# A decoder layer with eight experts on one core: the experts' units numbered the other way, w2 loaded in rows of 8 KB, the first layer's weights standing with a step of eight, and some stores and row copies moved to ScalarE

## What is computed

```python
x = x + self_attention(layernorm(x))            # 16 heads of 16, 3-D rope, softmax over 256 keys, output matrix Wo
x = x + cross_attention(ctx, ctx, layernorm(x))  # keys and values straight from ctx, masked, output W_fc.T
x = x + ffn(layernorm(x))
# ffn, with 8 experts of 1024 units, and 4 "languages":
router_logits = x @ router_w.T + router_b + 0.1 * expert_weights(softmax(x @ lang_w.T + lang_b))
top_p, top_i  = top_k(softmax(router_logits), 2);  top_p = top_p / top_p.sum()
h             = gelu(einsum('bsd,edh->bseh', x, w1) + b1)      # 256 -> 1024, exact gelu
expert_out    = einsum('bseh,ehd->bsed', h, w2) + b2           # 1024 -> 256
ffn           = sum over the two chosen experts of top_p * expert_out
```

## Time and profile before

| | us |
|---|---|
| median of three runs | 744.08 |
| the three runs | 743.53, 744.08, 750.2 |
| the profiled execution, device time | 739.92 |
| its span, first to last instruction | 737.9 |
| TensorE busy in the span | 644.9 (87%) |
| mean granted clock | 0.942 |

### The profile page before, as it was taken

The page is one execution under the profiler, slowest core; times in us unless marked ns, Lnnn a source line. Parts: engine busy times, 40 slices in busy tenths (PEclk is TensorE's granted clock), DMA queues, the critical chain, the costliest instruction groups (busy, mean ns, idle before and its releaser), DMA issues.

```text
span 737.9 us, 15213 instructions
## 1 busy us (share of the span) xinstructions
PE 644.9 (87%) x4859; PEld 517.0 (70%) x4859; DVE 350.3 (47%) x812; ACT 405.3 (55%) x872; POOL 287.6 (39%) x543
## 2 busy tenths in 40 slices
PE   4576899798998998989876878979999999999996
PEld 3354576475765766666543567969999999999995
DVE  2276777587776886877772422511212121221211
ACT  3443658467575687778554663635454545455451
POOL 3232406335144345454164451552333333434322
PEclk9688999899999999999897898999999999999998
DMA  4535566646676477886978592132221222222122
GB/s 130 142 102 144 105 142 144 155 114 141 146 156 154 135 157 163 185 190 137 247 140 161 172 198 62 23 37 39 30 44 29 45 31 43 35 38 39 35 31 22
DMA packets 58173, 78.26 MB, mean 106 GB/s; under 512 B 13069, under 2 KB 51344, under 8 KB 55408
## 3 DMA queue, kind: packets, MB, share of 16 engines
q1 hardware_dynamic: 49128, 66.61, 39.2%
q0 software_dynamic: 8512, 10.26, 9.2%
q10 hardware_dynamic: 456, 0.42, 0.2%
HBM read 54.52 MB, written 22.35 MB: 104 GB/s over the span
## 4 chain that ended last, share of the span: by engine, by line
PE 64%; DMA 10%; POOL 7%; DVE 7%; issue 5%; ACT 3%; SPq 3%; ACTq 0%; POOLq 0%; DVEq 0%
PE attention_psum L701 17%; PE attention_psum L694 17%; PE attention_psum L686 6%; PE attention_psum L646 5%; PE attention_psum L733 5%; PE attention_psum L659 5%; PE attention_psum L595 3%; PE attention_psum L601 3%; DMA weights<-in_x 3%; DMA weights<-in_L_ffn_w 3%; DVE neg_max L1156 2%; POOL rstd L1323 2%; DMA weights<-maxT 2%; DMA out<-over 1%; POOL tmp L1323 1%
## 5 line engine op out<-in xcount | busy, mean ns | idle before, releaser
L1156 DVE TENSOR_REDUCE neg_max<-attention_psum 128x2 f32<-128x512 f32 x256 | 167.6, 683 | 63.4 <-PE attention_psum L646 62.8
L858 ACT ACTIVATE weights<-attention_psum 128x512 f32<-128x512 f32 x256 | 147.3, 596 | 81.7 <-PE attention_psum L659 80.6
L701 PE MATMUL attention_psum<-weights 128*128 x624 | 143.7, 384 | 6.4 <-issue 6.4
L694 PE MATMUL attention_psum<-over,v 128*128 128x128 f32 x1248 | 147.8, 277 | 0.0
L694 PEld LDWEIGHTS attention_psum<-over,v 128*128 128x128 f32 x1248 | 144.5, 194 | 0.2
L945 ACT ACTIVATE weights<-attention_psum,b_sb 128x128 f32<-128x128 f32 x312 | 89.3, 369 | 83.6 <-PE attention_psum L694 83.6
L701 PEld LDWEIGHTS attention_psum<-weights 128*128 128x128 f32 x624 | 117.4, 193 | 21.5 <-issue 6.6
L1420 POOL DMA_INDIRECT out<-over x39 | 63.0, 1616 | 166.1 <-DVE over L1214 155.2
L646 PE MATMUL attention_psum<-weights 99*128 99x256 bf16 x512 | 102.8, 284 | 19.8 <-DVE neg_max L1156 13.2
L1208 DVE TENSOR_TENSOR over<-attention_psum,b_sb 128x256 f32<-128x256 f32 x39 | 16.6, 425 | 207.3 <-PE attention_psum L701 206.7
L659 PE MATMUL attention_psum<-weights 102*128 102x256 bf16 x512 | 101.9, 283 | 5.7 <-DMA weights<-maxT 5.3
(11 more groups left out here) (163 smaller groups left out, 709.3 us busy)
## 6 DMA issues: line engine op xcount, KB each, us to landing
parts<-weights SPq DMA_DIRECT2D x96, 128.0 KB
weights<-parts SPq DMA_DIRECT2D x28, 384.0 KB
weights<-in_L_ffn_w SPq DMA_DIRECT2D x8, 1024.0 KB, 12.2
weights<-parts SPq DMA_DIRECT2D x28, 256.0 KB
weights<-parts SPq DMA_DIRECT2D x36, 128.0 KB, 3.2
w_sb<-in_L_ffn_w SPq DMA_DIRECT2D x8, 512.0 KB, 3.7
weights<-in_L_ffn_w SPq DMA_DIRECT2D x8, 512.0 KB, 9.0
weights<-in_x SPq DMA_DIRECT2D x8, 256.0 KB, 8.2
```

Of the source, the lines that this page charges most:

```text
L694: last = pe.matmul(m.hT_bank[j % 2][:, c * P:(c + 1) * P], m.w1t[j % 2][:, k, c * P:(c + 1) * P], m.xT[j % 2][:, k, :], start=(k == 0), st ...
L701: last = pe.matmul(m.bank_of(("down_a", TILE, j))[:, 0:D], m.hidT[j % 2][:, c, :], m.w2_sb[:, bass.ds(expert, 1), c, :].rearrange("p a n - ...
L858: act.activation(m.p[:, u % P_RING, :], m.b_bank[u % B_RING], ACT.Exp, scale=SCALE[ORDER[u // H][0]]).then_inc(m.b_free[u % B_RING], 1)
L1156: v.tensor_reduce(m.neg_max[:, :, h:h + 1], m.a_bank[u % A_RING].rearrange("p (t k) -> p t k", t=T), AXX, ALU.max, negate=True).then_inc(m ...
```

## The change

- **Numbering of the units.** Unit 8 p + c of the expert's first layer is now on partition p in group c, not 128 c + p. w2 is so loaded in one row of 8 KB per partition. In `up`, the standing block is `w1t[:, k, c::8]`: 128 columns that stand 32 bytes apart. b1 is loaded straight into `b1_sb` (8 runs of 32 B per partition); the `b1` piece on TensorE and VectorE goes.
- **Who issues.** The two stores behind the third layer norm are issued by ScalarE, right behind the norm. The `max_rows` copies of the units 13 to 15 (`OWN_ROWS`) are issued by ScalarE too, right behind its copy to `maxT`; those of the units before stay with SP.
- **Nine tiles.** `EARLY` is 9: tile 8 is also made of rows of the first four batches.
- **Three buffers of `hidT`.** The third lies over x rows that have been stored; gelu of tile n waits for `down` of tile n - 3, and once for the stores of the second batch.
- **Places.** Nearly every table has other slots. The last three units have a table each (`LAST_AT`). The last w2 load stands in slot 272, ahead of two others in slot 276.
- **Order of waits on TensorE.** A piece waits for its PSUM bank first and for its data second. `warm` could put idle matmuls between the two; `WARM` asks for 0 of them, so there are none.
- A read of a stack's second half (`w` = 1) waits for the free stack as the first does.

```diff
-EARLY = 8
+EARLY = 9
...
-STACKS = 3
+STACKS, HIDDEN = 3, 3
+
+OWN_ROWS = 13
...
-        0), (-18, "v", 1))
-CROSS_AT = ((-35, "cx"), (-32, "ln_a", 1), (-26, "keys"), (-25, "ln_d", 1), (-17, "vcross"))
...
+        0), (-15, "v", 1))
+CROSS_AT = ((-38, "cx"), (-32, "ln_a", 1), (-29, "keys"), (-24, "ln_d", 1), (-20, "vcross"))
...
-BOTH_AT = ((-20, "stack", 0), (-19, "rest", 0), (-18, "mid", 0), (-17, "stack", 1), (-17, "rest", 1), (-17, "write", 0),
-        (-16, "mid", 1), (-14, "write", 1), (-12, "read", 0), (-12, "read", 1), (10, "max_parts", 0), (11,
-        "max", 0), (11, "max_rows", 0), (15, "max_parts", 1), (18, "max", 1), (20, "max_rows", 1))
...
+BOTH_AT = ((-19, "stack", 0), (-19, "rest", 0), (-18, "mid", 0), (-17, "stack", 1), (-17, "rest", 1), (-17, "write", 0),
+        (-16, "mid", 1), (-16, "write", 1), (-12, "read", 0), (-7, "read", 1), (10, "max_parts", 0), (11, "max",
+        0), (11, "max_rows", 0), (15, "max_parts", 1), (18, "max", 1), (20, "max_rows", 1))
...
-FIXED_AT = (-26, -9, 8)
...
+FIXED_AT = (-26, -8, 8)
...
+LAST_AT = (((-34, "cx"), (-32, "ln_a", 1), (-28, "ln_d", 1), (-23, "keys"), (-21, "stack", 0), (-20, "stack", 1), (-19,
+        "rest", 0), (-19, "rest", 1), (-18, "mid", 0), (-17, "vcross"), (-17, "write", 0), (-16, "mid", 1),
+        (-13, "write", 1), (-12, "read", 0), (-12, "read", 1), (8, "max_parts", 0), (10, "max", 0), (11,
+        "max_rows", 0), (15, "max_parts", 1), (17, "max", 1), (22, "max_rows", 1), (31, "o_move", 0), (38,
+        "o_move", 1), (38, "ot", 0), (39, "ot", 1), (43, "cturn"), (47, "proj_a"), (48, "proj"), (52, "ln_a",
+        2), (56, "ln_d", 2), (57, "rturn"), (58, "logits")), ((-37, "cx"), (-32, "ln_a", 1), (-26, "ln_d", 1),
+        (-24, "keys"), (-20, "stack", 0), (-19, "rest", 0), (-19, "stack", 1), (-18, "mid", 0), (-18, "vcross"),
...
+WARM = ((0, "stack", 1, 3, 0),)
+AFTER_SELF = ((17, "xbias"),)
...
-W1_AT, W1_EVERY, W2_AT = 231, 3, (243, 249, 249, 264, 263, 276, 275, 277)
+W1_AT, W1_EVERY, W2_AT = 231, 3, (246, 251, 249, 264, 262, 276, 276, 272)
...
-TILES_AT = ((258, "list", 0), (261, "list", 1), (261, "list", 2), (261, "list", 3), (262, "w1t", 0), (264, "list", 4),
...
+TILES_AT = ((258, "list", 0), (261, "list", 1), (261, "list", 2), (262, "w1t", 0), (264, "list", 3), (264, "list", 4),
         (264, "list", 5), (264, "list", 6), (264, "gather", 0), (264, "gather", 1), (264, "gather", 2), (267,
...
+        "down_a", 2), (300, "moved_y", 1), (300, "w1t", 4), (301, "add", 1), (301, "up_b", 3), (302, "down_b",
+        2), (303, "gather", 7), (303, "list", 8), (303, "moved_y", 2), (303, "add", 2), (305, "gather", 8))
...
-    slots[12 * H + 12].pieces.append(("b1", SELF, 0))
...
-        for table, lag in (((SELF_AT, CROSS_AT)[a], 0), (BOTH_AT, 0), ((AFTER_SELF, AFTER_CROSS)[a], LAG), (AFTER, LAG)):
-            if table is AFTER_CROSS and n + 1 in BATCH_ENDS:
-                table = table + AFTER_BATCH[batch_of(n)[0]]
+        tables = (((SELF_AT, CROSS_AT)[a], 0), (BOTH_AT, 0), ((AFTER_SELF, AFTER_CROSS)[a], LAG), (AFTER, LAG))
+        if POS[unit] >= len(ORDER) - len(LAST_AT):
+            tables = ((LAST_AT[POS[unit] - len(ORDER)], 0),)
+        for table, lag in tables:
             for at, *piece in table:
                 if z >= 2 * H or at + lag >= 0:
                     put(at + lag, *piece)
+        if a == CROSS and n + 1 in BATCH_ENDS:
+            for at, *piece in AFTER_BATCH[batch_of(n)[0]]:
+                put(at + LAG, *piece)
         if a == CROSS and n + 1 in BATCH_ENDS:
             b, tiles = batch_of(n)
             for t in range(tiles.start, tiles.stop):
...
+        self.warm = {tuple(piece): many for many, *piece in WARM}
...
+        self.hidT.append(self.xs[:, 0:2 * T, :].rearrange("p t (c q) -> p (t c) q", q=P))
...
-                sp.dma_start(m.b1_in[:, :], b1.rearrange("e (c p) -> (e c) p", p=P)).then_inc(m.s_b, 16)
+                sp.dma_start(m.b1_sb[:, :, :], b1.rearrange("e (p c) -> p e c", c=FC)).then_inc(m.s_b, 16)
...
-                if w == 0 and i >= STACKS:
+                if i >= STACKS:
                     u = (i - STACKS + 1) * H - 1
                     sp.wait_ge(m.b_full[u % B_RING], u // B_RING + 1)
-                if w == 0 and i < STACKS:
+                if i < STACKS:
...
-            elif name == "max_rows":
+            elif name == "max_rows" and i < OWN_ROWS:
...
-            elif name == "ln_d" and piece[3] == 2:
-                sp.wait_ge(m.s_normed[2], n + 1)
-                sp.dma_start(out_t[:, n * T:(n + 1) * T, :], m.rows_of(n)).then_inc(m.stored(m.s_out, n)[0], 16)
-                sp.dma_start(rows_t[:, n * T:(n + 1) * T, :], m.rows_sb[:, :, :]).then_inc(m.stored(m.s_rows, n)[0], 16)
...
-                sp.dma_start(m.w2_sb[:, n, :, :], w2[n].rearrange("(c p) d -> p c d", p=P)).then_inc(m.s_w2, 16)
+                sp.dma_start(m.w2_sb[:, n, :, :], w2[n].rearrange("(p c) d -> p c d", c=FC)).then_inc(m.s_w2, 16)
...
+    wide = m.identb[:, :].rearrange("p (a d) -> p a d", a=1).broadcast_to([P, BANK // P, P])
...
-        return m.bank_of(piece)
-
-    def turn_rows(piece, rows):
-        bank = fill(piece)
+        bank = m.bank_of(piece)
+        warm(piece, bank)
+        return bank
+
+    def warm(at, bank):
+
+        for _ in range(plan.warm.get(at, 0)):
+            pe.matmul(bank[:, :], m.identb[:, :], wide, start=True, stop=True)
+
...
+        bank = m.a_bank[u % A_RING]
+        if u >= A_RING:
+            pe.wait_ge(m.a_free[u % A_RING], u // A_RING)
+        if h % HALF == 0:
+            warm(("top", i, h // HALF), bank)
...
-        if u >= A_RING:
-            pe.wait_ge(m.a_free[u % A_RING], u // A_RING)
-        bank = m.a_bank[u % A_RING]
...
-                last = pe.matmul(m.hT_bank[j % 2][:, c * P:(c + 1) * P], m.w1t[j % 2][:, k, c * P:(c + 1) * P],
+
+                last = pe.matmul(m.hT_bank[j % 2][:, c * P:(c + 1) * P], m.w1t[j % 2][:, k, c::FC],
                                  m.xT[j % 2][:, k, :], start=(k == 0), stop=(k == KC - 1))
...
-            last = pe.matmul(m.bank_of(("down_a", TILE, j))[:, 0:D], m.hidT[j % 2][:, c, :],
+            last = pe.matmul(m.bank_of(("down_a", TILE, j))[:, 0:D], m.hidT[j % HIDDEN][:, c, :],
...
-            elif name == "b1":
-                pe.wait_ge(m.s_b, 16)
-                pe.transpose(fill(piece)[:, 0:E * FC], m.b1_in[:, :],
-                             m.ident[0:E * FC, 0:E * FC]).then_inc(m.fills(piece), 1)
...
+        if k == 2:
+            act.wait_ge(m.s_normed[2], n + 1)
+            act.dma_start(out_t[:, n * T:(n + 1) * T, :], src).then_inc(m.stored(m.s_out, n)[0], 16)
+            act.dma_start(rows_t[:, n * T:(n + 1) * T, :], dst[:, :, :]).then_inc(m.stored(m.s_rows, n)[0], 16)
...
-                        act.wait_ge(*m.emptied(("b1", SELF, 0)))
+                        act.wait_ge(m.s_b, 16)
                         act.wait_ge(m.s_values, len(ORDER) * H)
                     gelu_expert = act.value_load(m.tile_expert[0:1, n:n + 1], min_val=0, max_val=E - 1)
-                    if n > 1:
-                        act.wait_ge(m.s_down, n - 1)
+                    if n == HIDDEN - 1:
+                        act.wait_ge(*m.stored(m.s_out, BATCH_ENDS[0] + 1))
+                    if n >= HIDDEN:
+                        act.wait_ge(m.s_down, n - HIDDEN + 1)
...
-                    last = act.activation(m.hidT[n % 2][:, c, :], m.hT_bank[n % 2][:, c * P:(c + 1) * P], ACT.Gelu,
+                    last = act.activation(m.hidT[n % HIDDEN][:, c, :], m.hT_bank[n % 2][:, c * P:(c + 1) * P], ACT.Gelu,
...
+                if i >= OWN_ROWS:
+                    act.wait_ge(*m.emptied(piece))
+                    for part in range(PARTS):
+                        act.dma_start(m.stack[i % STACKS][0][MAX0 + part:MAX0 + part + 1, half * HALF:(half + 1) * HALF],
+                                      m.maxT[half][part * HALF:(part + 1) * HALF]).then_inc(m.s_max_rows[half], 16)
...
-            elif name == "b1":
-                v.wait_ge(*m.filled(piece))
-                v.tensor_copy(m.b1_sb[:, :, :].rearrange("p e c -> p (e c)"),
-                              m.bank_of(piece)[:, 0:E * FC]).then_inc(m.frees(piece), 1)
```

95 lines of the change are left out of this document (55 added, 40 removed).

## The result

The changed kernel takes 890.91 us, the median of 4 runs (885.61 to 895.83), beside 744.08 us for the kernel before. The ratio is 1.1984, with a 95% interval of 1.1922 to 1.2046. The forecast was 726 us, in a range of 706 to 742. The profiled execution took 895.83 us with a span of 893.8, against 739.92 and 737.9 before: 155.9 us more of each.

The account below looks back on a forecast made before the run. TensorE was taken to bound the steady expert tiles, with gains only in waits elsewhere: 6.8 + 9.0 + 6.4 - 4 = 18.2 us off 744.08 gave 725.9, said as 726 us, range 706 to 742.

Parts of the forecast that it names:

- w1 standing with a step of eight: Weight loads of `up`: strided columns might cost 0 to 85 us over 1248 loads; taken as 0.
- is paced by its columns and not by what it fetches, and a longer step may find room: Weight loads: reason for 0, from 100 ns for 128 bf16 columns against 116 for float32.
- there is hardly room behind the matmuls to hide a slower load: Steady part of the expert stage: weight loads are already busy 37.46 of 40 us.
- Rival 1: Every weight load of `up`: strided weights cost, 85 us more, 811 us; chance 0.16.
- w2 in rows of 8 KB: Before the first `down`: 6.4 us wait and 2.6 of slow clock go, 9.0 us gained.
- issues moved to ScalarE: Attention: row maxima copies on ScalarE's queue gain 6.8 us; of ScalarE's 22 us of issuing, 4 show.
- nine early tiles: Tile 8's gather: 4.8 us wait and 1.6 of slow clock go, 6.4 us gained.
- places, hidT, b1, copies: New slots, third hidden buffer, `b1` piece: 0, with places in the first 15 units between -6 and +6 us.
- three loads 1.7 + 6 x 2.0 = 13.7: Last three w2 loads at the end of attention: 13.7 us instead of 21.0, landed at 437.3.
- Rival 2: Border of attention and experts: half or more of 9.0 + 6.8 us is lost, 736 us; chance 0.20.
- would land by 393.3 to 395.3: Row maxima for the last unit's first half: landing time on ScalarE's queue, before TensorE stood from 396.9 on.
- ScalarE was busy 39.55 of 50 us: Middle of attention: a fifth of slack, so of 22 us of issuing between 0 and 12 show; 4 taken.

Follow-up runs that it names:

- e1: Kernel before with only the standing block of `up` read with a step of eight; 887.53 us, ratio 1.1917.
- e2: Changed kernel, but the copies that fill `w1t` take the step and `up` reads 128 columns in a row; 735.68 us, ratio 0.9932.
- e4: Kernel before with the standing step of `up` set by tile to 1, 2, 4, 8 and 1 again; 785.05 us.
- e12: Kernel before with the standing step of `up` set by tile to 1, 3, 5, 6 and 1 again; 801.25 us.
- e5: e2 with the row copies of units 13 to 15 and each batch's stores issued by SP again; 732.91 us, ratio 0.9855.
- e10: e2 with general tables for the last three units and SP issuing all row copies and stores; 739.5 us, ratio 0.9969.
- e6: e2 with w2 loaded in eight rows of 1 KB per partition; 739.46 us, ratio 0.9950.
- e9: e2 with the last three units taking the general tables instead of their own; 745.42 us, ratio 1.0058.
- e8: e2 with `EARLY` back at 8 and tile 8's two pieces taken out of the earlier slots; 746.95 us, ratio 1.0028.
- e7: Kernel before with the new numbering alone, `w1t` copies as in e2, old slots, eight early tiles, SP issuing; 743.88 us, ratio 1.0011.
- e3: e2, but the copies into `w1t` read w1 in order and write with a step of 128 floats; 738.52 us, ratio 0.9892.
- e11: Kernel before with `down` reading its 256 moving columns of w2 with a step of eight; 887.06 us, ratio 1.1919.

## Why the prediction was wrong

**The step that failed** is "w1 standing with a step of eight ... the bounds are 0 and 85. I take 0." It cost 143 us in e1 (0.1917 of 744) and 153 in the changed kernel against e2, 1.7 to 1.8 times its own upper bound. What the runs showed in its place: TensorE pays 1.8 ns for each 16 bytes that it touches, so that a matmul whose 128 standing columns have 16 bytes each to themselves takes 238 ns instead of 112.

- The reason given for 0 was that a load "is paced by its columns and not by what it fetches, and a longer step may find room", from 100 ns for 128 bf16 columns against 116 for 128 float32 ones. Both stood in one piece, with at least four columns to 16 bytes. They show what sets the pace when fetching doesn't, and can't say from where on it does. The runs e4 and e12 show it: 64 pieces of 16 bytes are all but hidden, 96 and 128 are not.
- The same part had said that "there is hardly room behind the matmuls to hide a slower load". That was right, and counted for more than the argument that was preferred to it: 1248 instructions without cover multiply any error in the price of one.
- The upper bound was another engine's. VectorE's 0.53 ns a number stood for a pass that already takes 3.4 ns a number (220 / 64), its fixed cost included, so a slower fetch can be hidden in it. On ScalarE's copy (1.03 ns a column in a row) the step adds 0.98 ns a column, on VectorE's (0.68) 0.40, on TensorE's load 0.98. What a step adds on one engine is no upper bound for another.
- Rival 1 had the mechanism, the place and the sign, but 811 us for it (a tile of 9.4 us; measured 11.3) and a chance of 0.16.

The Trainium skill (SBUF — State Buffer, section Door 1: The DMA port swizzle) wants two hits in each 16-byte line, a hit being a read that falls into it. This is what the runs show for TensorE's standing operand: at step 2, two hits, 118 ns; at one hit a line 221 to 238. The moving operand was run at one hit a line alone, and there it pays the same (460 ns for 256 columns). Where the page goes on to say that four float32 are a step that is free, it differs from the run: step 4 costs as much as step 8, and the measurement decides. The prediction read a "step of eight is beyond it" out of that sentence and then let the rule weigh 0.16.

**The other terms,** by e2 and e5 to e10, with 744 us as the whole:

```
term                            forecast      measured
w2 in rows of 8 KB              -9.0          -1.3  (e2 against e6)
issues moved to ScalarE         -6.8 + 4      +5.7  (e2 against e5), +6.6 (e9 against e10)
nine early tiles                -6.4          -7.1  (e2 against e8)
places, hidT, b1, copies        0 (-6 to 6)   -2.4  (what is left)
sum without the step            -18.2         -5.1  (e2)
```

Each measured one is uncertain by 4 to 6 us, so the row of w2 says little more than that it isn't 9, and only e9 against e10 and the ninth tile (just) have intervals apart. The row of the places is what is left over, not a measurement.

- *w2.* The step that failed is "three loads 1.7 + 6 x 2.0 = 13.7". From the first of these issues to the last landing it took 15.5 to 19.6 us in the eight kernels with rows of 8 KB, and 17.1 to 21.3 in the six with rows of 1 KB. The wait goes with 8 KB rows and old places (e7) as well as with 1 KB rows and new places (e6), all but 0.3 us, but w2 stays nearly the last to come: the first `down` starts 1.07 to 1.11 us after its last landing in the kernel before and in e3, e5, e6, e7 and e9 alike. In those five TensorE waits there 1.0 us at most (e9), because it comes later or has an `up` to do meanwhile. Rival 2 ("the waits at the border move and don't go") describes this, and its 10 us of loss is about what is missing: 7.7 here.
- *Issues.* The copy of the row maxima no longer held TensorE up, as said, but by luck: that it "would land by 393.3 to 395.3" failed. In e2 it landed 8.3 us after its last issue, and TensorE came later still. The price of ScalarE's 22 us of issuing (19 in e2's trace) was put at 4. One group of issues among the exponentials of unit 12 already costs 3 to 4 us, and there are six groups. If the 6.8 were gained, a balance of +5.7 to +6.6 would make the price about 13; as the wait was exchanged, how the balance splits stays open. "ScalarE was busy 39.55 of 50 us" was read as slack, but an issue ahead of an exponential delays that exponential (2.23 us in the row of e5's section), and a slack of a fifth is spread over many small gaps. The Trainium skill (DMA: Bandwidth & Descriptors, section Issuing engines are not separate DMA queues) had warned that another issuer saves only issue time. The traces agree, with 3.7 to 8.9 us on ScalarE's queue inside the 1.7 to 12.4 on SP's, and here the issue time went to the engine which TensorE waits for.
- *Nine tiles.* Right in mechanism, and in size within what can be told (7.1 against 6.4).
- *Places.* The 0 hid two large terms: the last three units' own tables win 9.4 us (e2 against e9), so the other edits in that line would lose some 7. The dearer copies on ScalarE and VectorE may be part of it. And e10 with its ninth tile taken off, 0.9969 + 0.0096 = 1.0065, stands 0.0054 above e7, 4 us for general tables, slots of tiles and third buffer together, which is no more than the uncertainty of such a sum. Which of these loses isn't separated.

The reading of the steady part was right: the length of `up` and of a tile told the cause in one row of the timeline.

## What to carry to other kernels

Before a float32 operand of TensorE is read with a step, count the 16-byte pieces that it touches and multiply by 1.8 ns (as measured here at the full clock): if that passes the time that one matmul now takes, the step sets the pace, for the standing and the moving operand alike. Put the step into a copy on an engine with room (39 x 1.0 us on ScalarE and 39 x 0.4 us on VectorE here, against 153 us on TensorE), or order the data so that two columns share 16 bytes. And where an edit is paid 1248 times without cover and its price is unknown, the forecast should not rest on 0. An engine that others wait for is a dear place to issue DMAs from, even when it is idle a fifth of the time: ask which instruction stands behind each issue.

## What the runs showed of the hardware that was not expected

- TensorE reads float32 operands at 1.8 ns for each 16-byte piece, so that a matmul with 128 standing columns loses little with two columns to a piece (118 ns against 112) and takes twice the time with one, and the price of a piece is the same for them (233 to 238 ns) and for 256 moving columns (460 ns).
- Steps of 5 and 6 are 4 to 7% cheaper than 4 and 8 (221 and 223 against 233 and 238 ns), unexplained.
- ScalarE's copy of 1024 float32 columns takes 1058 ns in a row, 2060 read with a step of 8 and 1979 written with one of 128. VectorE's takes 694, 1099 and 1322.
- SP can stand for microseconds on the issue of one load when w2 comes in rows of 1 KB. In all six kernels with such rows (before, e1, e4, e6, e11, e12) a 512 KB load issued right behind w2 loads took SP 5.0 to 7.0 us to issue; with rows of 8 KB no issue of a weight load took over 1.6 us in any of the eight kernels. With the slots of the kernel before, the last three w2 loads took SP 3.9 to 6.2 us to issue with 1 KB rows (five kernels) and 1.29 with 8 KB (e7). The time of the whole kernel doesn't show it (e2 against e6).
- The three copies of 4 KB that the last unit's first half waits for took 1.7 to 12.4 us from issue to landing beside the weight loads, whichever engine issued them.
